# Transposes of two units share a pair of joined PSUM banks and one copy of 1024 columns

## The chip, the cores and the metric

The kernel runs on one core of a Trainium2 chip. A core has TensorE (PE in the profile; PEld is its weight load), VectorE (DVE), ScalarE (ACT), GpSimd (POOL) and SyncE (SP), which here only issues DMAs. Each engine runs its own list of instructions in order, and engines wait for one another by semaphores. The metric is the device time of one execution in microseconds (us); three runs of the kernel before gave 233.63, 234.40 and 234.79 us.

## The reference

Six residual layers on x, 16 batches x 32 tokens x 128 features: a local cross-attention, an RWKV-like recurrence, a small routed FFN, then the masked cross-attention in which the change lies, a linear attention with an FFN, and a mixture of 16 experts with a capacity. The masked cross-attention is, cut to its core:

```
qh, kh, vh = _split_heads(q @ Wq + bq), _split_heads(k @ Wk + bk), _split_heads(v @ Wv + bv)
scores = jnp.einsum('bhqd,bhkd->bhqk', qh, kh) * scale     # 16 batches, 16 heads, 32 queries, 512 keys
scores = scores + mask * NEG
weights = jax.nn.softmax(scores, axis=-1)
out = jnp.einsum('bhqk,bhkd->bhqd', weights, vh)
return out.transpose(0, 2, 1, 3).reshape(...) @ Wo + bo    # 128 features
```

## The kernel before, in words

**Units.** The cross-attention is cut into 64 units: 16 batches of 4 groups, each unit 4 heads x 32 queries (128 rows) by 512 keys. A unit goes through six steps:

- S, scores (L1406, PE): one matmul of 512 columns; a turn of the stream does the four units of a batch, into banks 0, 1, 2 and 5.
- least (L955, DVE): mask added, minimum taken, written to one of 8 tiles in SBUF.
- exponentials (L580, ACT): exp in place with its sum.
- T, turns (L1420, PE): four transposes of 128x128 into one PSUM bank, bank 3 for even units and bank 4 for odd ones.
- copies (L591 on ACT, L966 on DVE): the bank of 512 columns to one of 8 tiles `pt` in SBUF. Of every 8 units in turn, DVE copies those at 1, 4 and 7 and ACT the other five, so DVE copies 24 and ACT 40 in all.
- V, outputs (L1436, PE): 16 small matmuls for a batch, once its four units are copied.

The transposes of unit u wait for its exponential and for the copy of unit u-2, the last one that read the same bank. A copy waits for the transposes of its own unit, and for the batch whose V last read the `pt` tile. Before the cross-attention banks 3 and 4 serve the 32 projections of keys and values (L1235, L1239) in turn, and the first transposes wait until the last of these is copied.

**Order.** Every engine's list is woven from streams (Python generators): L the local attention, P the projections, a and b the two halves of the small layers, S, T and V as above (on DVE S is least, on ACT it is the exponentials, and T the copies on both), c and d the two halves of the later layers with the experts, G filler matmuls (L1650) that keep TensorE occupied near the end. `TURNS` is a table with one string for each engine: "T3" takes three turns of stream T. A turn of a stream that has ended does nothing. So the table decides what stands between two instructions of an engine, and nothing else does.

Of the kernel before, what the change touches and what calls it, by code (L numbers as in the profile page):

```python
# [6 lines left out]
F32 = mybir.dt.float32  # L7
# [4 lines left out]
P = 128  # L12
# [40 lines left out]
def columns(pack):  # L53

    at, out = 0, {}
    for name, n in pack:
# [10 lines left out]

TURNS = {
# [7 lines left out]
    "DVE": (  # L76
# [6 lines left out]
    "ACT": (  # L83
# [4 lines left out]
    "POOL": (  # L88
        "L2 a5 b a3 b a4 b10 c3 d c L a d c a c d2 L c d b d c b2 d b L a2 c L d2 ")}

# [26 lines left out]
def program(nc, x_d, early_d, next_d, late_d, ctx_d, ctok_d, mask_d, w1_d, w2_d, moeb_d, out_d):  # L117
    with ExitStack() as stack:
# [5 lines left out]
        def sig(name):  # L124
            if name not in sems:
                sems[name] = stack.enter_context(nc.semaphore(name))
            return sems[name]


        bank = [stack.enter_context(nc.psum_tensor(f"bank{i}", [P, 512], F32)) for i in range(8)]  # L130


        early, following, late = sb("early", width(EARLY)), sb("following", width(NEXT)), sb("late", width(LATE))
# [154 lines left out]

        def copied(j):

            part, n = j % 8, j // 8
            mine = part in BY_DVE
            before = sum(1 for k in range(part + 1) if (k in BY_DVE) == mine)
            return ("pT_dve", len(BY_DVE) * n + before) if mine else ("pT_act", (8 - len(BY_DVE)) * n + before)

        BY_DVE = (1, 4, 7)

        def taker(i):

# [172 lines left out]
        def _(act):  # L472
# [110 lines left out]

            def copies():

                for j in range(2 * UNITS):
                    if copied(j)[0] == "pT_act":
                        act.wait_ge(sig("pT_ps"), j + 1)
                        if j >= NPT:
                            act.wait_ge(sig("o1_ready"), (j - NPT) // GROUPS + 1)  # L590
                        s.copy(pt[j % NPT], bank[TB[j % 2]][:, :]).then_inc(sig("pT_act"), 1)  # L591
                        yield

            def linear_stages(h):
# [52 lines left out]
        def _(dve):  # L647
# [310 lines left out]

            def copies():

                for j in range(2 * UNITS):
                    if copied(j)[0] == "pT_dve":
                        dve.wait_ge(sig("pT_ps"), j + 1)
                        if j >= NPT:
                            dve.wait_ge(sig("o1_ready"), (j - NPT) // GROUPS + 1)
                        v.tensor_copy(pt[j % NPT], bank[TB[j % 2]][:, :]).then_inc(sig("pT_dve"), 1)  # L966
                        yield

            def take_heads():
# [226 lines left out]
        def _(pe):  # L1196
# [213 lines left out]
            def turns():  # L1410

                for u in range(2 * UNITS):
                    pe.wait_ge(sig("p1_ready"), u + 1)
                    if u < 2:
                        name, n = taker(len(PROJ) - 2 + u)
                    else:
                        name, n = copied(u - 2)
                    pe.wait_ge(sig(name), n)
                    for k in range(KT):
                        last = nc.tensor.transpose(bank[TB[u % 2]][:, P * k:P * (k + 1)], sc[u % NSC][:, P * k:P * (k + 1)], wt("ident"))  # L1420
                    last.then_inc(sig("pT_ps"), 1)
                    yield

            def outputs():

                for b in range(BATCH):
                    for j in range(GROUPS * b, GROUPS * (b + 1)):
                        name, n = copied(j)
                        pe.wait_ge(sig(name), n)
                    if b % 4 == 0 and b >= 4:  # L1430
# [323 lines left out]
```

## Time and profile before

| | us |
|---|---|
| median of three runs | 234.40 (233.63 to 234.79) |
| profiled execution | 233.0 |
| its span, first to last instruction | 231.2 |
| PE busy, share of the span | 217.0, 94% |
| DVE busy | 176.3, 76% |
| ACT busy | 131.7, 57% |
| granted TensorE clock, mean | 1.000 |

The span is 1.8 us shorter than the time of the same execution. The units of the cross-attention run from 89.2 us (the first S) to 181.4 us (the end of the last V), 92 of the 231 us; around and between them stand streams a and b up to about 133 us and stream c from about 136 us on. After them comes stream d, 50 us of small dependent steps.

### The profile page before, as it was taken

Reading aid. Unit: us, or ns where it says so; the run is one execution under the profiler, and the core shown is the slowest. Engines: PE = TensorE matmul, PEld = TensorE weight load, DVE = VectorE, ACT = ScalarE, POOL = GpSimd, SP = SyncE. Lnnn points to the kernel's source line nnn. Section 1 sums busy time; section 2 is a strip of 40 time slices with the busy share of each in tenths; the row PEclk is TensorE's granted clock in tenths of the full one; section 3 lists DMA queues with packets and bytes.
Section 4 is the critical chain, followed back from the end, with each engine's and each line's share of the span. In section 5 each row is a group of like instructions: output and inputs, shape, how many; then the busy total and the mean of one; then the engine's idle time right before and its main releaser. Section 6 shows DMA issues by size and latency. Waiting matters only on the chain.

```text
span 231.2 us, 5285 instructions
## 1 busy us (share of the span) xinstructions
PE 217.0 (94%) x1996; PEld 155.2 (67%) x1996; DVE 176.3 (76%) x507; ACT 131.7 (57%) x292; POOL 34.7 (15%) x55
## 2 busy tenths in 40 slices
PE   7999999999999998689899999999999989799995
PEld 6432785666876887355477766767677778688495
DVE  2476825999865799998798889999989777825672
ACT  2303452354488164889999979879969720123030
POOL 2020001050205137202050230020001031210000
DMA  6999979400000000007000520000009999200001
GB/s 217 396 420 463 403 292 230 89 3 0 4 0 0 3 0 1 0 3 181 3 0 4 135 52 0 3 3 1 3 3 346 404 428 412 96 0 0 3 3 45
DMA packets 2905, 26.88 MB, mean 116 GB/s; under 512 B 448, under 2 KB 704, under 8 KB 1344
## 3 DMA queue, kind: packets, MB, share of 16 engines
q1 hardware_dynamic: 2880, 26.54, 31.6%
q8 instruction: 16, 0.26, 0.5%
q14 instruction: 9, 0.07, 0.1%
HBM read 26.28 MB, written 0.26 MB: 115 GB/s over the span
## 4 chain that ended last, share of the span: by engine, by line
PE 74%; DVE 13%; issue 6%; ACT 3%; POOL 1%; POOLq 0%; DVEq 0%
PE bank L1420 11%; PE bank L1296 6%; PE bank L1274 6%; PE bank L1406 6%; PE bank L1436 5%; PE bank L1235 5%; PE bank L1239 3%; DVE ctx_sb L955 3%; PE bank L1246 2%; PE bank L1219 2%; PE bank L1650 2%; PE bank L1362 2%; PE bank L1379 2%; PE bank L1641 2%; PE bank L1263 2%
## 5 line engine op out<-in xcount | busy, mean ns | idle before, releaser
L580 ACT ACTIVATE ctx_sb<-ctx_sb,small_sb 128x512 f32<-128x512 f32 x64 | 45.9, 721 | 2.9 <-DVE small_sb L955 2.7
L955 DVE CUSTOM_DVE_ANT_0 ctx_sb<-bank,mask_sb 128x512 f32<-128x512 f32 x64 | 41.8, 682 | 2.6 <-PE bank L1406 1.4
L1420 PE MATMUL bank<-early_sb,ctx_sb 128*128 128x128 f32 x256 | 36.6, 278 | 2.8 <-DVE work_sb L966 1.8
L1420 PEld LDWEIGHTS bank<-early_sb,ctx_sb 128*128 128x128 f32 x256 | 28.0, 141 | 16.5 <-ACT ctx_sb L580 8.0
L382 POOL TENSOR_TENSOR rstd_sb<-veps_sb,minus_half_sb 128x2 f32<-128x2 f32 (+1 forms) x15 | 11.0, 734 | 125.7 <-DVE veps_sb L675 125.7
L591 ACT COPY work_sb<-bank 128x512 f32<-128x512 f32 x40 | 23.0, 580 | 8.1 <-PE bank L1420 8.0
L1406 PE MATMUL bank<-k_sb,work_sb 32*128 32x512 f32 x128 | 18.2, 638 | 2.3 <-DVE small_sb L955 1.8
L723 DVE SCALAR_TENSOR_TENSOR work_sb<-bank,early_sb,work_sb 128x512 f32<-128x512 f32 x16 | 11.8, 747 | 8.5 <-PE bank L1274 8.0
L1239 PEld LDWEIGHTS bank<-late_sb,ctx_sb 128*128 128x128 f32 x128 | 15.5, 191 | 3.4 <-issue 3.3
L1436 PE MATMUL bank<-work_sb,v_sb 128*32 128x128 f32 x512 | 17.1, 275 | 0.1
L1235 PE MATMUL bank<-ctx_sb,early_sb 128*128 128x512 f32 x32 | 16.3, 607 | 0.0
L966 DVE COPY work_sb<-bank 128x512 f32<-128x512 f32 x24 | 16.3, 681 | 0.1
L1239 PE MATMUL bank<-late_sb,ctx_sb 128*128 128x128 f32 x128 | 16.3, 278 | 0.0
L1274 PE MATMUL bank<-ctx_sb,early_sb 128*128 128x512 f32 x32 | 16.0, 605 | 0.3 <-DVE work_sb L723 0.2
L495 ACT ACTIVATE k_sb<-bank,early_sb 128x512 f32<-128x512 f32 x12 | 8.0, 685 | 14.1 <-PE bank L1235 14.1
L1436 PEld LDWEIGHTS bank<-work_sb,v_sb 128*32 128x32 f32 x512 | 13.2, 109 | 3.4 <-issue 1.7
L514 ACT COPY work_sb<-bank 128x512 f32<-128x512 f32 x16 | 9.3, 585 | 7.9 <-PE bank L1296 7.9
L580 ACT ACTIVATION_READ_ACCUMULATOR ctx_sb<-ctx_sb,small_sb 128x1 f32 x64 | 12.4, 193 | 0.0
L484 ACT ACTIVATE lnT_sb<-bank 128x256 f32<-128x256 f32 (+1 forms) x7 | 2.9, 413 | 14.4 <-PE bank L1205 14.3
L322 DVE TENSOR_TENSOR work_sb<-bank,early_sb 128x512 f32<-128x512 f32 x16 | 10.3, 678 | 0.8 <-PE bank L1283 0.7
L1650 PE MATMUL bank<-early_sb 128*128 128x128 f32 x64 | 10.0, 284 | 0.0
L1274 PEld LDWEIGHTS bank<-ctx_sb,early_sb 128*128 128x128 f32 x32 | 5.2, 189 | 6.5 <-issue 6.3
(264 smaller groups left out, 396.7 us busy)
## 6 DMA issues: line engine op xcount, KB each, us to landing
k_sb<-moe_w SPq DMA_DIRECT2D x1, 4096.0 KB, 13.5
ctx_sb<-moe_w SPq DMA_DIRECT2D x1, 4096.0 KB, 16.9
ctx_sb<-ctx SPq DMA_DIRECT2D x3, 1024.0 KB, 14.5
late_sb<-late SPq DMA_DIRECT2D x1, 2966.5 KB, 20.8
mask_sb<-ctx_tok SPq DMA_DIRECT2D x1, 2048.0 KB, 12.9
v_sb<-ctx_tok SPq DMA_DIRECT2D x1, 2048.0 KB, 28.2
mask_sb<-mask SPq DMA_DIRECT2D x4, 512.0 KB, 7.9
mask_sb<-mask SPq DMA_DIRECT2D x8, 256.0 KB, 4.5
```

The costliest lines, as they stand in the source:

```text
L580: s.activation(sc[u % NSC], sc[u % NSC], ACT.Exp, bias=smin[:, u:u + 1], scale=-1.0, accum_out=rsum[:, u:u + 1]).then_inc(sig("p1_ready"), 1)
L591: s.copy(pt[j % NPT], bank[TB[j % 2]][:, :]).then_inc(sig("pT_act"), 1)
L955: v.tensor_tensor_reduce(sc[u % NSC], bank[SB[u % GROUPS]][:, :], mask[:, KEYS * b:KEYS * (b + 1)], MASK_BIG, 3e38, ALU.add, ALU.min, smin ...
L966: v.tensor_copy(pt[j % NPT], bank[TB[j % 2]][:, :]).then_inc(sig("pT_dve"), 1)
L1235: last = mm(dst[:, :], wt("wk1"), ctx[:, KEYS * b:KEYS * (b + 1)], start=True, stop=True)
L1239: last = mm(dst[:, P * k:P * (k + 1)], ctx[:, at:at + P], wt("wv1"), start=True, stop=True)
L1274: mm(bank[c % 2][:, :], wt("wk0"), ctx[:, KEYS * c:KEYS * (c + 1)], start=True, stop=True).then_inc(sig("k0_ps"), 1)
L1296: last = mm(bank[c % 2][:, P * k:P * (k + 1)], ctok[h][:, at:at + P], mix[c % NE][:, P * k:P * (k + 1)], start=True, stop=True)
L1406: mm(bank[SB[g]][:, :], qc[b][r, :], k1[r, KEYS * b:KEYS * (b + 1)], start=True, stop=True)\
L1420: last = nc.tensor.transpose(bank[TB[u % 2]][:, P * k:P * (k + 1)], sc[u % NSC][:, P * k:P * (k + 1)], wt("ident"))
L1436: last = mm((bank[OB2][r, 0:P] if b == BATCH - 1 else bank[OB1][r, at:at + P]), vkey[:, b, k, r], pt[(GROUPS * b + g) % NPT][:, P * k:P * ...
L1650: mm(bank[2][:, 0:P], wt("ident"), early[:, 0:P], start=True, stop=True)
```

## The change

Banks 3 and 4 are allocated as one tensor `bank34` of 1024 columns, with the old names as its two halves. Two units (an even one and the next) form a pair. The transposes of the pair fill both halves; one operation of 1024 columns copies both to two neighbouring `pt` tiles. The choice of the copying engine goes by pairs: of 8 pairs in turn DVE takes those at 1, 4 and 6, so DVE has 12 copies and ACT 20. The first transposes of a pair wait for the copy of the pair before it; a copy waits for the transposes of both units. All four strings of `TURNS` are new.

```diff
 TURNS = {
     "PE": (
-        "P a2 b a3 b P2 b P b a P a P2 S L P2 S T5 S T V T b T S T3 V b T b S L T2 b S T b T V2 b T b S b T2 "
+        "b P a3 b P2 b P b a P a P2 S P2 S a T2 a T2 S T P T V T b T S T2 V T2 P b S b T2 V S T2 b2 V T b T b "
...
-        bank = [stack.enter_context(nc.psum_tensor(f"bank{i}", [P, 512], F32)) for i in range(8)]
+        bank = [stack.enter_context(nc.psum_tensor(f"bank{i}", [P, 512], F32)) for i in range(3)]
+        twin = stack.enter_context(nc.psum_tensor("bank34", [P, 1024], F32))
+        bank += [twin[:, 0:512], twin[:, 512:1024]]
+        bank += [stack.enter_context(nc.psum_tensor(f"bank{i}", [P, 512], F32)) for i in range(5, 8)]
...
         def copied(j):
-            part, n = j % 8, j // 8
+            part, n = j // 2 % 8, j // 16
...
-        BY_DVE = (1, 4, 7)
+        BY_DVE = (1, 4, 6)
...
             def copies():                                       # on ACT; on DVE likewise
-                for j in range(2 * UNITS):
+                for j in range(0, 2 * UNITS, 2):
                     if copied(j)[0] == "pT_act":
-                        act.wait_ge(sig("pT_ps"), j + 1)
+                        act.wait_ge(sig("pT_ps"), j + 2)
                         if j >= NPT:
-                            act.wait_ge(sig("o1_ready"), (j - NPT) // GROUPS + 1)
-                        s.copy(pt[j % NPT], bank[TB[j % 2]][:, :]).then_inc(sig("pT_act"), 1)
+                            act.wait_ge(sig("o1_ready"), (j + 1 - NPT) // GROUPS + 1)
+                        s.copy(tile(7 + j % NPT, 2), twin[:, :]).then_inc(sig("pT_act"), 1)
...
             def turns():
                 for u in range(2 * UNITS):
                     pe.wait_ge(sig("p1_ready"), u + 1)
-                    if u < 2:
-                        name, n = taker(len(PROJ) - 2 + u)
-                    else:
-                        name, n = copied(u - 2)
-                    pe.wait_ge(sig(name), n)
+                    if u % 2 == 0:
+                        for name, n in (copied(u - 2),) if u else (taker(len(PROJ) - 2), taker(len(PROJ) - 1)):
+                            pe.wait_ge(sig(name), n)
...
             def outputs():
                 for b in range(BATCH):
-                    for j in range(GROUPS * b, GROUPS * (b + 1)):
+                    for j in range(GROUPS * b, GROUPS * (b + 1), 2):
                         name, n = copied(j)
                         pe.wait_ge(sig(name), n)
```

What the new table puts on TensorE, first in the dense middle of the cross-attention, from the transposes of the 13th pair on. L1420 is a transpose (L1421 after), L1406 a score matmul (L1409), L1436 a V matmul (L1437), L1388 one matmul of stream b (L1391). Before:

```order
L1388 MATMUL bank7<-lnT_sb,late_sb 128x256
L1420 MATMUL bank4<-early_sb,ctx_sb 128x128 x4
L1420 MATMUL bank3<-early_sb,ctx_sb 128x128 x4
L1436 MATMUL bank6<-work_sb,v1_sb 32x128 x16
L1406 MATMUL bank0<-k1_sb,work_sb 128x512
L1406 MATMUL bank1<-k1_sb,work_sb 128x512
L1406 MATMUL bank2<-k1_sb,work_sb 128x512
L1406 MATMUL bank5<-k1_sb,work_sb 128x512
L1420 MATMUL bank4<-early_sb,ctx_sb 128x128 x4
L1420 MATMUL bank3<-early_sb,ctx_sb 128x128 x4
L1420 MATMUL bank4<-early_sb,ctx_sb 128x128 x4
L1436 MATMUL bank6<-work_sb,v1_sb 32x128 x16
```

and after:

```order
L1391 MATMUL bank7<-lnT_sb,late_sb 128x256
L1421 MATMUL bank34<-early_sb,ctx_sb 128x128 x8
L1409 MATMUL bank0<-k1_sb,work_sb 128x512
L1409 MATMUL bank1<-k1_sb,work_sb 128x512
L1409 MATMUL bank2<-k1_sb,work_sb 128x512
L1409 MATMUL bank5<-k1_sb,work_sb 128x512
L1421 MATMUL bank34<-early_sb,ctx_sb 128x128 x8
L1437 MATMUL bank6<-work_sb,v1_sb 32x128 x16
L1421 MATMUL bank34<-early_sb,ctx_sb 128x128 x8
```

Before, up to three units are transposed in a row, with the banks in turn; after, pairs of units alternate with one S or one V.

The second place is the end of the cross-attention on TensorE, behind the last S: L1525/L1526, L1219/L1222, L1205/L1208 and L1538/L1539 are steps of stream c. Before:

```order
L1406 MATMUL bank5<-k1_sb,work_sb 128x512
L1420 MATMUL bank3<-early_sb,ctx_sb 128x128 x4
L1219 MATMUL bank7<-late_sb,mask_sb 128x128 x2
L1420 MATMUL bank4<-early_sb,ctx_sb 128x128 x4
L1436 MATMUL bank6<-work_sb,v1_sb 32x128 x32
L1420 MATMUL bank3<-early_sb,ctx_sb 128x128 x4
L1420 MATMUL bank4<-early_sb,ctx_sb 128x128 x4
L1205 MATMUL bank7<-early_sb,xn_tok_sb 128x128 x2
L1420 MATMUL bank3<-early_sb,ctx_sb 128x128 x4
L1420 MATMUL bank4<-early_sb,ctx_sb 128x128 x4
L1538 MATMUL bank7<-lnT_sb,late_sb 128x256 x2
```

and after:

```order
L1437 MATMUL bank6<-work_sb,v1_sb 32x128 x16
L1421 MATMUL bank34<-early_sb,ctx_sb 128x128 x4
L1526 MATMUL bank7<-early_sb,mask_sb 128x128 x2
L1421 MATMUL bank34<-early_sb,ctx_sb 128x128 x4
L1222 MATMUL bank7<-late_sb,mask_sb 128x128 x2
L1421 MATMUL bank34<-early_sb,ctx_sb 128x128 x8
L1437 MATMUL bank6<-work_sb,v1_sb 32x128 x16
L1421 MATMUL bank34<-early_sb,ctx_sb 128x128 x4
L1208 MATMUL bank7<-early_sb,xn_tok_sb 128x128 x2
L1421 MATMUL bank34<-early_sb,ctx_sb 128x128 x4
L1539 MATMUL bank7<-lnT_sb,late_sb 128x256 x2
L1421 MATMUL bank34<-early_sb,ctx_sb 128x128 x8
```

The last S now stands earlier, with ten units still to transpose behind it instead of six, and between the last pairs stand L1222, one V and L1539.

## Rows read from the trace of the kernel before

**Rows 1.** The page: busy time of each engine, and the chain that ended last.
```profile
PE 217.0 (94%) x1996; PEld 155.2 (67%) x1996; DVE 176.3 (76%) x507; ACT 131.7 (57%) x292; POOL 34.7 (15%) x55
...
PE 74%; DVE 13%; issue 6%; ACT 3%; POOL 1%; POOLq 0%; DVEq 0%
```

**Rows 2.** Busy us (xinstructions) by stretch: PE, PEld, DVE, ACT, POOL, then clock.
```profile
90.00:100.00 10.00, 7.52 (x56) 4.58 (x52) 10.00 (x25) 7.15 (x18) 4.05 (x5) 1.00 0.01 2
100.00:110.00 10.00, 8.83 (x116) 6.29 (x112) 9.21 (x29) 8.76 (x24) 1.32 (x2) 1.00 0.43 105
110.00:120.00 10.00, 9.01 (x111) 5.95 (x111) 8.83 (x33) 9.90 (x20) 2.91 (x1) 1.00 0.01 2
120.00:130.00 10.00, 9.93 (x73) 7.38 (x72) 8.30 (x27) 9.58 (x23) 0.07 (x1) 1.00 0.05 11
130.00:140.00 10.00, 9.63 (x147) 7.12 (x144) 8.96 (x25) 8.72 (x22) 3.41 (x4) 1.00 0.42 100
140.00:150.00 10.00, 10.00 (x135) 7.04 (x137) 9.82 (x31) 9.15 (x26) 0.00 (x0) 1.00 0.01 2
150.00:160.00 10.00, 10.00 (x128) 7.29 (x132) 9.45 (x30) 8.54 (x23) 1.38 (x2) 1.00 0.01 2
160.00:170.00 10.00, 10.00 (x108) 6.57 (x108) 9.24 (x25) 9.23 (x25) 0.00 (x0) 1.00 0.01 2
170.00:180.00 10.00, 9.61 (x156) 7.63 (x148) 9.29 (x30) 7.65 (x19) 0.70 (x1) 1.00 0.55 211
```

**Rows 3.** The chain that ended last, in order: start us, us, what.
```profile
139.28 1.02 PE bank L1420 x8
140.30 1.07 PE bank L1406 x8
141.37 0.59 PE bank L1420 x4
141.96 1.01 PE bank L1436 x32
142.97 0.43 PE bank L1449 x8
...
146.97 0.45 PE bank L1462 x4
```

**Rows 4.** Groups by line: xcount | busy us, mean ns | idle before.
```profile
L591 ACT COPY work_sb<-bank 128x512 f32<-128x512 f32 x40 | 23.0, 580 | 8.1 <-PE bank L1420 8.0
L966 DVE COPY work_sb<-bank 128x512 f32<-128x512 f32 x24 | 16.3, 681 | 0.1
```

**Rows 5.** One line each: min/median/max ns of the nearest other widths.
```profile
L600 ACT COPY mask_sb<-bank x1: 372/372/372, 189.8 to 189.8; 128x256 f32<-128x256 f32 x1
L620 ACT ACTIVATE mask_sb<-mask_sb x1: 1057/1057/1057, 184.3 to 184.3; 128x1024 f32<-128x1024 f32 x1
L1065 DVE COPY mask_sb<-bank x2: 415/420/424, 172.8 to 194.8; 128x256 f32<-128x256 f32 x2
```

**Rows 6.** Timeline: start us, us, engine, line, what, [idle before <-releaser].
```profile
101.64 0.68 DVE L966 COPY work_sb<-bank 128x512 f32<-128x512 f32 x1
...
102.47 0.63 PE L1420 MATMUL bank<-early_sb,ctx_sb 128*128 128x128 f32 x4 [0.80 <-DVE work_sb L966]
...
136.91 0.59 ACT L591 COPY work_sb<-bank 128x512 f32<-128x512 f32 x1 [0.40 <-PE bank L1420]
...
137.64 0.63 PE L1420 MATMUL bank<-early_sb,ctx_sb 128*128 128x128 f32 x4 [0.33 <-ACT work_sb L591]
...
138.30 0.59 ACT L591 COPY work_sb<-bank 128x512 f32<-128x512 f32 x1 [0.81 <-PE bank L1420]
138.78 0.73 ACT L580 ACTIVATE ctx_sb<-ctx_sb,small_sb 128x512 f32<-128x512 f32 x1
...
140.36 0.68 DVE L966 COPY work_sb<-bank 128x512 f32<-128x512 f32 x1
...
140.96 0.41 DVE L998 TENSOR_TENSOR mask_sb<-late_sb,small_sb 128x256 f32<-128x256 f32 x1
...
148.80 1.09 PE L1420 MATMUL bank<-early_sb,ctx_sb 128*128 128x128 f32 x8
...
150.18 0.66 DVE L966 COPY work_sb<-bank 128x512 f32<-128x512 f32 x1
```

**Rows 7.** Timeline: the short steps of stream c, and the last V.
```profile
155.79 0.65 PE L1470 MATMUL bank<-lnT_sb,late_sb 128*128 128x256 f32 x2
...
156.27 0.61 PE L1219 MATMUL bank<-late_sb,lnT_sb 128*128 128x128 f32 x4
...
182.25 1.10 PE L1538 MATMUL bank<-lnT_sb,late_sb 128*128 128x256 f32 x4 [0.17 <-ACT mask_sb L615]
...
183.18 0.61 PE L1457 MATMUL bank<-late_sb 128*128 128x128 f32 x4
```

**Rows 8.** What PE waited for, 120 to 181 us: us, times, longest.
```profile
PE bank L1420 <- DVE work_sb L966: 0.3, 1, 0.3
PE bank L1420 <- ACT work_sb L591: 0.3, 1, 0.3
```

More of the change, by code:

```diff
@@ L69 @@
     "PE": (
[6 rows of a table removed]
-    "DVE": (
[6 rows of a table removed]
[6 rows of a table added]
+    "DVE": (
[6 rows of a table added]
     "ACT": (
[4 rows of a table removed]
[4 rows of a table added]
     "POOL": (
-        "L2 a5 b a3 b a4 b10 c3 d c L a d c a c d2 L c d b d c b2 d b L a2 c L d2 ")}
+        "L a L a5 b a2 b a3 b a b L b5 L b3 c2 b L c d a L c d c d c d a b d a c2 d c L b c a b d b d3 a ")}
 class Shifted:
@@ L959, in copies @@
             def copies():
-                for j in range(2 * UNITS):
+                for j in range(0, 2 * UNITS, 2):
                     if copied(j)[0] == "pT_dve":
-                        dve.wait_ge(sig("pT_ps"), j + 1)
+                        dve.wait_ge(sig("pT_ps"), j + 2)
                         if j >= NPT:
-                            dve.wait_ge(sig("o1_ready"), (j - NPT) // GROUPS + 1)
-                        v.tensor_copy(pt[j % NPT], bank[TB[j % 2]][:, :]).then_inc(sig("pT_dve"), 1)
+                            dve.wait_ge(sig("o1_ready"), (j + 1 - NPT) // GROUPS + 1)
+                        v.tensor_copy(tile(7 + j % NPT, 2), twin[:, :]).then_inc(sig("pT_dve"), 1)
                         yield
```

30 rows, old and new, of the table TURNS are left out of this document.

## The prediction, made before the changed kernel ran

> **What bounds the kernel now.** I read the page first. PE is busy for 94% of the span and holds 74% of the chain that ended last [rows 1]. Such an average hides that stages differ, so next come the stretches of 10 us in the 92 us of cross-attention [rows 2]. From 90 to 120 us PE is idle for 2.48 + 1.17 + 0.99 = 4.6 us, while DVE is full in the first of the three: this part hangs on stream b's recurrence. From 120 to 180 us PE is idle for 0.07 + 0.37 + 0.39 = 0.8 us in all. DVE (8.3 to 9.8 of 10) and ACT (7.7 to 9.6) are close behind, but the chain shows which ends last: PE follows PE with no wait between [rows 3]. So from 120 us on TensorE is the bound, and time in which it stands before a transpose is lost. Whatever delays the last V delays stream d, whose first steps take its result. The granted clock is 1.00 in every stretch [rows 2], TensorE's upper level of 2.4 GHz, and the change takes no filler away.
>
> **The change, part by part.**
>
> *Copies.* The trace has no copy of 1024 columns, so I bound it. On ACT 256 columns take 0.372 us and 512 take 0.580, 0.21 for 256 more, so 1024 should take 0.58 + 0.42 = 1.00; the one ACT operation of 1024 columns took 1.06 [rows 4, 5]. On DVE 0.420 and 0.681 give 0.681 + 0.52 = 1.20. Between that and two copies lie 1.00 to 1.16 for ACT and 1.20 to 1.36 for DVE; below these an operation would have to run faster per column than any row of its engine. I take 1.01 and 1.21, near the slopes. By durations that saves ACT 20 x (1.16 - 1.01) = 3.0 us and DVE 12 x (1.36 - 1.21) = 1.8 us. The engines gain less: the next exponential starts 0.48 us after a copy of 0.59 starts, the next DVE operation 0.60 after a copy of 0.68 [rows 6], so the last 0.1 us lies beside the next operation anyway. In engine time a pair saves 2 x 0.48 - (1.01 - 0.11) = 0.06 on ACT and 2 x 0.60 - (1.21 - 0.08) = 0.07 on DVE, 1.2 and 0.8 us in all. About four DVE copies lie where DVE bounds: -0.3 us. The rest goes to engines that don't end last.
>
> The Trainium skill (Perfetto Trace Analysis, Optimizing Scalar/DVE Operations) advises larger operations where the engine is saturated, with a busy overhead on PSUM of some 125 ns for DVE and 51 ns for ScalarE. By it, as an estimate, DVE would gain 12 x 0.125 = 1.5 us and ACT 20 x 0.051 = 1.0 us; the trace agrees on ACT and shows about half of it on DVE.
>
> *The banks.* This is the costly part. Before, unit u waits for the copy of u-2, so a copy lies beside the transposes of the unit between. After, both banks are held until one long copy is done, and only S, V and the small streams can fill the gap. Eight transposes take PE 1.02 us up to the next step [rows 3]; the last one ends 1.09 us after the first starts (the eight at 148.80) and a free copier starts 0.03 us behind that (137.64 + 0.63 to 138.30) [rows 6]. PE resumes 0.14 us behind an ACT copy (137.50 to 137.64) and 0.15 behind one of DVE (102.32 to 102.47) [rows 6]. From the first transpose of a pair to the first of the next it takes at least 1.09 + 0.03 + 1.01 + 0.14 = 2.27 us by ACT, 1.09 + 0.03 + 1.21 + 0.15 = 2.48 by DVE. So the gap between two pairs must hold 2.27 - 1.02 = 1.25 us of other PE work with ACT and 1.46 with DVE. S gives 1.07 and V 1.01 [rows 3]: S alone is short by 0.18 with ACT and 0.39 with DVE, V alone by 0.24 and 0.45.
>
> The new PE order has 31 such gaps. Fourteen hold enough (S and V together, or one with work of b or c). The first five are empty, S, V, S, V with copiers ACT, DVE, ACT, ACT, DVE: 1.25 + 0.39 + 0.24 + 0.18 + 0.45 = 2.5 us short. They lie at about 95 to 110 us, where PE idles 4.6 us for stream b; I count them as hidden, and as +2.5 if that cover is gone. The other twelve lie behind 125 us:
> - S alone, twice with ACT and three times with DVE: 0.36 + 1.17;
> - V alone, four times with ACT: 0.96;
> - L1391 alone, with ACT; its cover is 0.48 us as of L1470's row [rows 7]: 0.77;
> - L1222 alone, with DVE; 0.45 us as of L1219, here 156.27 to 156.72: 1.01;
> - L1539 alone, with DVE; 0.93 us as of L1538, 182.25 to 183.18 [rows 7]: 0.53.
>
> The sum is 4.8 us, of which the 0.8 us that PE was idle there before may take its part: +4.0. A step of PE that stands alone costs a bit more than in a row: a lone unit takes 0.59 us, two together 1.02 [rows 3], 0.07 less for each. By the two orders nine lone units behind 125 us become four: -0.3 us.
>
> *End of the cross-attention.* The last V needs the last pair's copy, and behind the last S there are now ten units instead of six. PE's total work is the same, so I cost this at nothing beyond the gaps above, which include the last two. Streams L, P, a, the first S and all of d have the same work in almost the same order; I take 0, and +-1 us for an order made anew.
>
> Sum: -0.3 + 4.0 - 0.3 = +3.4; on the profiled execution's own 233.0 that is 236.4 us. The median of the runs is 1.4 above that execution, so I forecast 234.4 + 3.4 = 237.8.
>
> The skill's same page (Matmuls) says that independent groups should rotate through PSUM banks so that the evacuation of one lies beside the next group's matmuls. The trace agrees in its copies that lie beside transposes. By this rule a pair without rotation loses its whole copy, minus what else PE has to do, which is the sum above.
>
> **Rivals.**
>
> *Faster: the copies were the bound.* From 140 to 170 us DVE is 92 to 98% busy and ACT 85 to 92% [rows 2], and PE's place in the chain may hang on how they keep up. If what ends last is DVE's queue and the new order puts enough S and V into the gaps, the whole 1.8 us of durations come off: 234.4 - 1.8 = 232.6, at most 3.0 by ACT's share, 231.4. It decides if PE stands before transposes no longer than before. For it: the balance of the three engines, and 4.6 us of PE idle that another order could use. Against it: PE has no wait in the chain from 139 to 147 us [rows 3], and engine time gains less than durations.
>
> *Much slower: the copier is not free.* Copies stand in order behind exponentials of 0.72 us or a DVE operation. Before, the DVE copy behind the eight transposes at 148.80 started at 150.18, 0.29 us after their end at 149.89 [rows 6]. With two banks this cost nothing; now each of the twelve gaps pays it: 12 x 0.3 = 3.6 more, 241.3.
>
> *No change: the gaps are covered.* If PE's idle 0.8 us, the first third's 4.6 and the relief of DVE and ACT take up the gaps, it stays at 234.4. That also holds if the loop of transposes and copies is seldom the last wait, because the exponential of the pair comes later than the copy of the one before.
>
> **How the numbers follow.** Forecast, +1.2 to +5: 0.42. Copier not free: 0.20. No change: 0.13. Faster: 0.25. About 0.5% (1.2 us) is what a measurement can tell from no change. So faster 0.25, same 0.13, slower 0.62. The likeliest case alone has 235.6 to 239.5. The range reaches into both others: down to 231.8, which takes in most of the faster case, and up to 242.0, past 241.3.
>
> **What would show it.** Right: PE idle time before the transposes, released by the copies, grows from 0.3 + 0.3 us behind 120 us [rows 8] to 4 or more, the largest before lone L1391, L1222 and L1539; copies of 1.01 and 1.21 us; the last V ends 3 us later, and stream d takes 50 us as before. Wrong: PE idles no more than before in that stretch; or copies start late, and the gaps are 0.3 us longer each; or the first five gaps come on top of stream b's idle time; or the last V comes on time and the end moves by stream d.

## The result, and the profile after

The changed kernel takes 240.84 us (median of four runs, 239.24 to 242.41), the kernel before beside it 234.59 (four runs, 233.63 to 239.77). The ratio is 1.028, 95% interval 1.019 to 1.037. The forecast was 237.8 us, range 231.8 to 242.0: the sign and the range were right, the size was 3 us too small (2.2 us at equal clock, below).

One thing must be known to read the sizes. Executions of either kernel differ in TensorE's mean granted clock, and the time goes with it (1.00 stands for 0.999 and more, 0.993 for 0.992 and 0.993): over the runs beside the experiments the kernel before has a median of 234.1 us at 1.00 (23 runs, 232.8 to 234.9), 235.9 at 0.993 (20 runs) and 237.9 at 0.978 (13 runs). At 1.00 the changed kernel has 239.7 (five runs, 239.2 to 240.3), which is 5.6 us over before; at 0.993 it has 241.5 (three runs, 241.4 to 242.4), again 5.6 over, where the forecast had 3.4. Single runs at one clock spread by 1 to 2 us, so differences of such medians are good to about 1 us, not to tenths. Below, "at 1.00" means such runs alone. The profiled execution of after has 0.993, that of before 1.00.

The page of the changed kernel, the lines of [rows 1] and [rows 4] (columns as there):

```profile
PE 222.8 (93%) x2008; PEld 158.4 (66%) x2008; DVE 177.0 (74%) x495; ACT 131.1 (54%) x272; POOL 34.5 (14%) x55
...
PE 57%; DVE 21%; issue 12%; ACT 4%; DMA 3%; POOL 2%; SPq 0%; DVEq 0%; POOLq 0%
...
L1421 PE MATMUL bank<-early_sb,ctx_sb 128*128 128x128 f32 x256 | 35.0, 277 | 5.0 <-ACT work_sb L594 2.7
...
L594 ACT COPY work_sb<-bank 128x1024 f32<-128x1024 f32 x20 | 20.1, 1006 | 10.6 <-PE bank L1421 10.4
...
L969 DVE COPY work_sb<-bank 128x1024 f32<-128x1024 f32 x12 | 14.7, 1222 | 1.2 <-PE bank L1421 1.1
```

The copies are cheaper in busy time, 20.1 us on ACT instead of 23.0 and 14.7 on DVE instead of 16.3. But the chain is no longer three quarters PE: DVE's share of it went from 13 to 21%, and the issue share from 6 to 12%. The copiers wait longer for PE before their copies, ACT 10.4 us instead of 8.0 [rows 4] for half as many copies, DVE 1.1 instead of next to nothing: they are not late themselves.

What PE waited for, 120 to 190 us (us, times, longest), beside [rows 8]:

```profile
PE bank L1421 <- ACT work_sb L594: 1.2, 5, 0.5
...
PE bank L1421 <- DVE work_sb L969: 1.1, 3, 0.6
```

Before it was 0.3 + 0.3 us; now it is 2.3. (This is less than what the gaps cost, as shown below the experiments.) The next view is the timeline of after where three pairs follow each other with one S or V between:

```profile
140.89 1.06 PE L1421 MATMUL bank<-early_sb,ctx_sb 128*128 128x128 f32 x8
...
141.89 1.08 PE L1437 MATMUL bank<-work_sb,v_sb 128*32 128x128 f32 x32
142.00 1.01 ACT L594 COPY work_sb<-bank 128x1024 f32<-128x1024 f32 x1 [0.18 <-PE bank L1421]
...
143.15 1.06 PE L1421 MATMUL bank<-early_sb,ctx_sb 128*128 128x128 f32 x8 [0.18 <-ACT work_sb L594]
...
144.26 1.22 DVE L969 COPY work_sb<-bank 128x1024 f32<-128x1024 f32 x1 [0.88 <-PE bank L1421]
...
145.40 0.34 DVE L994 RECIPROCAL small_sb<-small_sb 128x32 f32<-128x32 f32 x1
...
145.63 1.06 PE L1421 MATMUL bank<-early_sb,ctx_sb 128*128 128x128 f32 x8 [0.34 <-DVE work_sb L969]
```

From transposes to transposes it is 143.15 - 140.89 = 2.26 us where ACT copies and 145.63 - 143.15 = 2.48 where DVE does; the forecast had 2.27 and 2.48. DVE even stood idle 0.88 us for the transposes, and stream c's reciprocal (L994, L991 before) was queued behind that copy.

Where the 9.4 us between the two profiled spans went is best read from stretches cut at the same events in each: first projection, first S, L1388 of stream b's last part (L1391 after), last S, last V, end. Each row has the stretch, its length, then busy us (xinstructions) of PE, PEld, DVE, ACT, POOL, the granted clock, and the DMA share with GB/s. Before:

```profile
6.42:89.16 82.74, 81.96 (x497) 53.77 (x497) 59.87 (x141) 38.30 (x73) 13.30 (x26) 1.00 0.44 158
89.16:132.60 43.44, 38.72 (x396) 26.40 (x396) 39.42 (x121) 38.36 (x88) 10.54 (x10) 1.00 0.17 42
132.60:172.30 39.70, 39.34 (x508) 28.07 (x508) 37.21 (x109) 33.66 (x87) 3.45 (x4) 1.00 0.05 11
172.30:180.55 8.25, 7.85 (x108) 5.87 (x108) 7.86 (x26) 7.62 (x19) 0.70 (x1) 1.00 0.82 320
180.55:231.20 50.65, 44.11 (x480) 37.19 (x480) 30.28 (x105) 12.23 (x26) 4.85 (x7) 1.00 0.35 147
```

and after:

```profile
8.64:92.64 84.00, 82.83 (x496) 53.35 (x497) 59.93 (x137) 38.35 (x73) 13.00 (x20) 1.00 0.41 149
92.64:137.30 44.66, 39.65 (x393) 27.61 (x393) 38.20 (x115) 36.95 (x79) 10.42 (x10) 0.96 0.17 41
137.30:175.60 38.30, 35.49 (x436) 24.65 (x436) 34.30 (x97) 31.55 (x73) 3.45 (x4) 1.00 0.05 11
175.60:190.59 14.99, 13.63 (x179) 10.03 (x180) 11.75 (x32) 11.99 (x25) 0.70 (x1) 1.00 0.75 296
190.59:240.60 50.01, 45.40 (x492) 38.42 (x492) 30.29 (x105) 10.78 (x22) 4.84 (x7) 1.00 0.27 112
```

- 2.2 us lie ahead of the first projection, which waits for the first context DMA: 8.64 against 6.42. In the other profiled executions it starts at 6.8 to 8.4 us, with old and new tables, so at least part of this is this execution's own.
- 1.26 us lie between first projection and first S, before any transpose of the cross-attention.
- 6.56 us lie between first S and last V (97.95 against 91.39). PE's idle time in it, length less busy, rises from 4.72 + 0.36 + 0.40 = 5.48 to 5.01 + 2.81 + 1.36 = 9.18 us, by 3.7.
- The tail is 0.64 us shorter.

The busy time of the same stretch rises by 2.9 us with 1,008 records against 1,012. About 1 us of this is the clock. Sixteen matmuls of stream b (L1382) took the time below in a stretch at 0.87, where the same step (L1379) had 2.2 us in the execution before. But the run rotate below, with the same table and records and a clock of 1.00, has 38.56 + 35.30 + 13.89 = 87.75 us of busy time against 85.91 before: 1.8 us come with the new order, in which TensorE's steps lie less tightly behind each other. After also has 12 more matmul records than before, all of them filler (L1650), in the last 50 us.

```profile
129.47 3.56 PE L1382 MATMUL bank<-late_sb,mask_sb 128*128 128x128 f32 x16
```

### The profile page after: what moved, and what is told of

It reads as the page before. It is cut to its first block, busy times and chain, and to the rows that moved or that the text cites. A ratio compares the mean times of both kernels' runs of the same rounds, so it can differ in the third digit from the quotient of the medians.

```text
span 240.6 us, 5201 instructions
## 1 busy us (share of the span) xinstructions
PE 222.8 (93%) x2008; PEld 158.4 (66%) x2008; DVE 177.0 (74%) x495; ACT 131.1 (54%) x272; POOL 34.5 (14%) x55
## 4 chain that ended last, share of the span: by engine, by line
PE 57%; DVE 21%; issue 12%; ACT 4%; DMA 3%; POOL 2%; SPq 0%; DVEq 0%; POOLq 0%
PE bank L1421 7%; PE bank L1299 6%; DVE ctx_sb L958 6%; PE bank L1409 5%; PE bank L1277 5%; PE bank L1238 4%; PE bank L1651 3%; DMA ctx_sb<-ctx 3%; ACT work_sb L594 2%; DVE work_sb L969 2%; PE bank L1539 2%; PE bank L1437 2%; PE bank L1552 2%; PE bank L1642 2%; PE bank L1308 2%
## 5 line engine op out<-in xcount | busy, mean ns | idle before, releaser
L1421 PEld LDWEIGHTS bank<-early_sb,ctx_sb 128*128 128x128 f32 x256 | 27.9, 141 | 18.9 <-issue 9.7
L1421 PE MATMUL bank<-early_sb,ctx_sb 128*128 128x128 f32 x256 | 35.0, 277 | 5.0 <-ACT work_sb L594 2.7
L594 ACT COPY work_sb<-bank 128x1024 f32<-128x1024 f32 x20 | 20.1, 1006 | 10.6 <-PE bank L1421 10.4
L1409 PE MATMUL bank<-k_sb,work_sb 32*128 32x512 f32 x128 | 18.5, 638 | 2.4 <-DVE small_sb L958 1.4
L1437 PE MATMUL bank<-work_sb,v_sb 128*32 128x128 f32 x512 | 17.3, 275 | 0.2 <-ACT work_sb L594 0.2
L969 DVE COPY work_sb<-bank 128x1024 f32<-128x1024 f32 x12 | 14.7, 1222 | 1.2 <-PE bank L1421 1.1
L1437 PEld LDWEIGHTS bank<-work_sb,v_sb 128*32 128x32 f32 x512 | 13.1, 109 | 2.8 <-issue 2.6
L517 ACT COPY work_sb<-bank 128x512 f32<-128x512 f32 x16 | 9.1, 585 | 7.8 <-PE bank L1299 7.8
L1651 PE MATMUL bank<-early_sb 128*128 128x128 f32 x76 | 10.8, 280 | 0.0
L1651 PEld LDWEIGHTS bank<-early_sb 128*128 128x128 f32 x76 | 9.7, 192 | 0.2
## 6 DMA issues: line engine op xcount, KB each, us to landing
mask_sb<-ctx_tok SPq DMA_DIRECT2D x1, 2048.0 KB, 14.7
```

Of the source, the lines that this page charges most:

```text
L594: s.copy(tile(7 + j % NPT, 2), twin[:, :]).then_inc(sig("pT_act"), 1)
L969: v.tensor_copy(tile(7 + j % NPT, 2), twin[:, :]).then_inc(sig("pT_dve"), 1)
L1409: mm(bank[SB[g]][:, :], qc[b][r, :], k1[r, KEYS * b:KEYS * (b + 1)], start=True, stop=True)\
L1437: last = mm((bank[OB2][r, 0:P] if b == BATCH - 1 else bank[OB1][r, at:at + P]), vkey[:, b, k, r], pt[(GROUPS * b + g) % NPT][:, P * k:P * ...
L1651: mm(bank[2][:, 0:P], wt("ident"), early[:, 0:P], start=True, stop=True)
```

## The experiments

Theory A: the loop through the held banks is the cost (the forecast's sum). Rival B: the new order costs, whatever the banks do. Rival C: an engine, DVE above all, is the bound. Intervals are of the ratio to before.

**after_again.** The changed kernel once more, beside the next three.

> The changed kernel once more, for the spread of its own runs and for the granted clock. In its first profile the first context slice landed about 2.2 us later than before, and the clock fell to 0.96 and 0.87 in two stretches around 120 to 140 us. If both are chance of that execution, this profile starts its projections at about 7.5 us as before, keeps clock 1.00 and ends near 237 us of span (time 239); if the late start belongs to the kernel, it shows again, with 240 us or more. In either case the cross-attention, first S to last V, takes 95 to 98 us instead of 91.4.

Measured: 239.89 us, ratio 1.021 (1.014 to 1.027). Its stretches repeat to 0.02 us (84.00, 44.64, 38.30, 14.99, 50.01), the clock's dip included. So the loss is steady; only the start of the first projection (7.76) moved. The dip came again, the late start only in part.

**rotate.** After's table and order; each pair is copied by two operations of 512 on one engine, and each bank is free after its own.

```diff
-                        s.copy(tile(7 + j % NPT, 2), twin[:, :]).then_inc(sig("pT_act"), 1)
+                        for i in (j, j + 1):
+                            act.wait_ge(sig("pT_ps"), i + 1)
+                            s.copy(pt[i % NPT], bank[TB[i % 2]][:, :]).then_inc(sig("pT_act"), 1)
...
-                    if u % 2 == 0:
...
+                    name, n = copied(u - 2) if u > 1 else taker(len(PROJ) - 2 + u)
+                    pe.wait_ge(sig(name), n)
```

> The new table of turns is kept word for word; each pair's copy of 1024 columns is made as two of 512 by the same engine, and the transposes of unit u wait for the copy of u-2 only, so the two banks rotate again. Theory (banks held through one long copy bound the pairs' loop): PE's waits before transposes released by copies fall from 4.7 us to under 1.5, the cross-attention shrinks by 3 to 5 us, and the time comes to 235 to 237. Rival (the new order itself is worse, the banks don't matter): 239 to 241, with the same length of cross-attention as the changed kernel.

**split_only.** The same two copies, but the banks stay a pair: no transpose before both copies are done.

```diff
-                        for name, n in (copied(u - 2),) if u else (taker(len(PROJ) - 2), taker(len(PROJ) - 1)):
+                        for name, n in (copied(u - 1),) if u else (taker(len(PROJ) - 2), taker(len(PROJ) - 1)):
```

> The new table is kept; each pair's copy is made as two operations of 512 columns, both after the transposes of both units, and PE waits for both as in the changed kernel: no rotation. It prices the single operation alone. By the rows before, ACT holds the pair 0.48 + 0.59 = 1.07 us instead of 1.01 and DVE 0.60 + 0.68 = 1.28 instead of 1.22: theory, 0.06 us more in each of some 17 short gaps, +1 us against the changed kernel, 240 to 242. A rival by which the wide operation is what helps (the durations of 3.0 and 1.8 us): +2 to +4 us.

Measured: rotate 238.74 us, ratio 1.013 (1.006 to 1.021), at 1.00 238.1 us (three runs, 238.0 to 239.4); split_only 244.33, ratio 1.027 (1.018 to 1.036), at 1.00 241.7 (two runs). Rotate lies between theory (235 to 237) and rival (239 to 241). So the joined copy over held banks costs 239.7 - 238.1 = 1.6 us, and with the copy cut in two and the banks still held it is 3.6: the one wide operation is worth 2.0 us as long as the banks are held. Split_only's timeline accounts for these 2.0, which the expectation put at 1. From transposes to transposes it is 2.38 us by ACT (141.35 to 143.73) and 2.60 by DVE (143.73 to 146.33), 0.12 more than in after: 0.06 for the longer copying, as expected, and 0.06 because the copy starts that much later. Over the 17 short gaps this is 2.0. But 4.0 of the 5.6 us stay when the banks rotate. Rotate's groups and stretches:

```profile
L1423 PE MATMUL bank<-early_sb,ctx_sb 128*128 128x128 f32 x256 | 35.9, 278 | 0.7 <-ACT work_sb L596 0.6
...
L1412 PE MATMUL bank<-k_sb,work_sb 32*128 32x512 f32 x128 | 18.6, 638 | 4.1 <-DVE small_sb L960 2.8 <-POOL work_sb L412 1.1
```

```profile
8.28:92.28 84.00, 82.83 (x497) 53.38 (x497) 59.92 (x137) 38.35 (x73) 13.00 (x20) 1.00 0.41 149
92.28:135.50 43.22, 38.56 (x393) 26.04 (x393) 38.43 (x119) 37.31 (x86) 10.42 (x10) 1.00 0.18 42
135.50:172.95 37.45, 35.30 (x437) 24.71 (x437) 34.45 (x103) 32.23 (x83) 3.45 (x4) 1.00 0.05 12
172.95:187.60 14.65, 13.89 (x178) 10.09 (x179) 11.84 (x34) 11.75 (x28) 0.70 (x1) 1.00 0.80 312
187.60:237.60 50.00, 45.37 (x492) 38.42 (x492) 30.25 (x105) 10.78 (x22) 4.85 (x7) 1.00 0.26 110
```

The transposes (L1423) hardly wait, 0.7 us against 2.8 before and 5.0 after. Yet PE's idle time from first S to last V is 4.66 + 2.15 + 0.76 = 7.57, still 2.1 over before: it stands before S instead (4.1 us, before 2.3), for the minimum of the batch before (L960) and for POOL. With the 1.8 us of busy time this makes the 3.9 us by which this stretch is longer than before. The front keeps its 84.00.

**old_order_pairs.** Before's table with joined banks and joined copies: a pair's copy stands in the turn in which before copied the pair's later unit on that engine, and DVE takes pairs 0, 3 and 6 of eight to fit that table. The main lines:

```diff
-        bank = [stack.enter_context(nc.psum_tensor(f"bank{i}", [P, 512], F32)) for i in range(8)]
+        twin = stack.enter_context(nc.psum_tensor("bank34", [P, 1024], F32))
...
-        BY_DVE = (1, 4, 7)
+        BY_DVE = (0, 3, 6)
```

> The table of the kernel before, with joined banks and one copy of 1024 columns for a pair; ACT and DVE take a pair's copy where they took the copy of its last unit of theirs, DVE the pairs 0, 3 and 6 of 8 (a third of its places needed a new owner). Theory: an order made for rotating banks has gaps emptier still, with pairs back to back, so it is slower than the changed kernel, 242 to 248. Rival (the banks cost nothing and the order made anew costs): 234 to 237.

Measured: 264.17 us, ratio 1.124 (1.116 to 1.132), at mean clocks of 0.961 to 0.974. The direction is theory's, the size is not: 16 us above its range of 242 to 248. Some of it is the clock, which no run of this kernel had at 1.00. PE's waits over the whole run, then its timeline in the middle:

```profile
PE bank L1421 <- ACT work_sb L594: 11.9, 12, 1.2
PE bank L1421 <- DVE work_sb L969: 9.8, 11, 1.7
```

```profile
137.85 1.06 PE L1421 MATMUL bank<-early_sb,ctx_sb 128*128 128x128 f32 x4
140.11 1.09 PE L1421 MATMUL bank<-early_sb,ctx_sb 128*128 128x128 f32 x4 [1.19 <-ACT work_sb L594]
```

An order made for rotating banks puts the next transposes right behind a pair; every such gap is empty and costs a whole copy, here 1.19 us. So the joined copy needs another order, and the new one brings its 21.7 us of bank waits down to 4.7. What this order costs by itself is the next question.

**old_front and new_front.** Old_front is after with before's table up to the first S on PE, DVE and ACT (POOL's string stays); new_front is before with after's front, likewise. Such a line of PE's table, in new_front:

```diff
-        "L P L P L11 P4 L P L8 P L2 a L P L2 a P L a2 L a L P L P L2 P6 a L P2 L P L2 a L a2 L P L P L2 a L a "
+        "L P L P L11 P4 L P L8 P L2 a L P L2 a P L a3 L2 P L2 P L P5 a P L P L3 a P L a L2 P a L2 a P2 a L a2 "
```

> The changed kernel, but on each engine the table up to its first turn of S is that of the kernel before; behind it stand the new table's turns that are not yet taken. In four profiles of kernels with the new front the first scores start 84.00 us after the first projection, in the kernel before 82.74. Theory (the new front alone costs 1.3 us): 82.7 again, and 1.3 us less than the changed kernel, 238.5. Rival (joined banks 3 and 4 slow the projections, or it is chance): 84.0 and 239.9.

> The kernel before, but on each engine the table up to its first turn of S is the new one. Mirror of the run before it: by the theory 84.0 us from the first projection to the first scores and 235.8 us of time against 234.5 to 235.5, ratio 1.005; by the rival 82.7 and no change.

Measured: old_front 239.23 us, ratio 1.019 (1.011 to 1.027), at 1.00 238.3 (three runs, 237.9 to 238.7); new_front 235.76, ratio 1.003 (0.998 to 1.008), at 1.00 235.1 (seven runs, 234.4 to 236.0). Taking the new front out of after gives back 1.4 us, putting it into before costs 1.0 (1.2 at 0.993, four runs). The interval of new_front's ratio holds 1, so alone it wouldn't prove the step; the two together do. The stretch from first projection to first S agrees: 84.00 with the new front in after, after_again and rotate, 83.94 in new_front, 82.74 in before. Old_front's own stretch can't be used, as its profiled execution had a clock dip there.

**rotate_old_front.** Rotate with before's front: new order of the rest alone.

> The kernel with rotating banks and the new table, with the old table's front. If the three parts simply add (front 1.3, rotation 1.2 to 2, the rest of the new order 2 to 4), this is 237.4 us, still slower than before by 0.8 to 1.5%, and what is left is the order of the cross-attention's second half. A rival by which the front and the rotation are all: 235, same as before.

Measured: 240.55 us, ratio 1.016 (1.005 to 1.028); five of its six runs had a clock of 0.993 or lower, three of them 0.979. The one at 1.00 took 236.4, 2.4 over before; the one at 0.993 is 3.4 over before's 235.9, and the three at 0.979 are 3.3 over its 237.9. The sum 5.6 - 1.2 - 1.6 = 2.8 lies between. So the rest of the new order costs 2.4 to 3.4 us.

**narrow_copy and narrow_copy_before.** Only the middle 256 of 1024 columns of a pair are copied (of 512, the middle 128 before); all instructions and waits stay.

```diff
-                        s.copy(tile(7 + j % NPT, 2), twin[:, :]).then_inc(sig("pT_act"), 1)
+                        s.copy(tile(7 + j % NPT, 2)[:, 384:640], twin[:, 384:640]).then_inc(sig("pT_act"), 1)
```

> The changed kernel with each pair's copy cut to the middle 256 of its 1024 columns (three quarters of the transposed weights are not copied); order and waits unchanged. The hold of the banks falls by about 0.6 us on ACT and 0.8 on DVE, and the copies' engine time by 12 and 9 us. Theory by which long copies on both banks are the larger part: -4 to -6 us, PE's idle time before transposes nearly gone, and the cross-attention shorter than with narrow copies in the kernel before. Rival (the new order ties TensorE to the minimum operation on DVE and to stream c): -2 to -3 us, with PE still waiting for the minimum before scores.

> The kernel before with each copy cut to the middle 128 of 512 columns, the same three quarters left out. TensorE has no wait in its chain from 120 to 172 us, so by the prediction's reading hardly anything is gained behind 120 us and at most 1 to 2 us in the first third: 233 to 234.5. If the copies' engine time bounded (the rival of the prediction), -5 us or more.

Measured: narrow_copy 236.42 us, ratio 1.006 (1.002 to 1.010), at 1.00 236.3 (seven runs, 234.8 to 236.6), 3.3 below after. Narrow_copy_before 233.80, ratio 0.996 (0.992 to 1.001), at 1.00 232.8 (three runs), 1.3 below before. ACT's copy of 256 columns has a mean of 0.369 us (x20), 0.64 less than the wide one; so the length of a copy is worth 2.0 us more in after than in before. The transposes' wait falls to 0.6 us, while S still waits for the minimum, as the rival had it. This agrees with rotate: what depends on how long the banks are held is some 2 us, and over 2 us are left even with short copies, of which the front is about half.

**narrow_least and narrow_least_before.** DVE's minimum over 256 of 512 columns, in after and in before.

```diff
-                    v.tensor_tensor_reduce(sc[u % NSC], bank[SB[u % GROUPS]][:, :], mask[:, KEYS * b:KEYS * (b + 1)], MASK_BIG,
+                    v.tensor_tensor_reduce(sc[u % NSC][:, 0:256], bank[SB[u % GROUPS]][:, 0:256], mask[:, KEYS * b:KEYS * b + 256], MASK_BIG,
```

> The changed kernel with the mask-and-minimum operation on DVE cut to 256 of its 512 columns (half of each unit's scores are left out); the rest as it is. DVE is relieved by 64 x 0.27 = 17 us and the scores' banks come free 0.27 us earlier each. Theory (the new order hangs on DVE where TensorE waits for the minimum before each S): -4 to -6 us. Rival (the copies are what holds TensorE): -2 us or less.

> The same cut in the kernel before. There TensorE bounds from 120 us on, so only the first third, where DVE carries stream b's recurrence, can gain: -2 to -3 us, less than in the changed kernel. If both gain alike, the dependence on DVE is no part of the difference.

Measured: narrow_least 237.85 us, ratio 1.011 (1.004 to 1.018), at 1.00 237.8 (three runs, 236.0 to 237.9), 1.9 below after. Narrow_least_before 235.34, ratio 0.997 (0.992 to 1.002); none of its runs had a clock of 1.00. At 0.992 to 0.993 it has a median of 233.4 (four runs, 233.0 to 234.7), 2.5 below before's 235.9. Both kernels win about 2 us from a faster DVE, so both hang on DVE in places, and rival C explains none of the difference. In narrow_least S no longer waits for the minimum; 0.6 us of waiting for POOL is left.

**rotate_tail.** The last look at the order: in rotate's table the last V stands 3.3 us behind stream c's L1538 (1.05 before). Here the last pair's transposes go ahead of that matmul and its copies ahead of ACT's table load.

```diff
-        "T2 c V T2 V T2 c S c T2 S c T2 c V L T c T P S c T S T V T P c T c S T2 V2 d c b d2 c d2 G d2 c b G2 "
+        "T2 c V T2 V T2 c S c T2 S c T2 c V L T c T P S c T S T V T2 c T2 c P S V2 d c b d2 c d2 G d2 c b G2 "
...
-        "c S4 T c3 T L c b S L P S3 P T S4 a T S4 b S T S c3 T S c4 T d2 c d2 b2 d c S d7 T c d P S T d6 c2 a "
+        "c S4 T c3 T L c b S L P S3 P T S4 a T S4 b S T S c T c2 S c4 T d2 c d2 b2 d c S d7 T c d P S T d6 c2 "
```

> The kernel of run rotate (the changed kernel's table, each joined pair copied out by two operations of 512 columns of one engine, banks rotating) with the last part of the table changed: on TensorE the last pair's transposes stand ahead of stream c's first FFN matmul (L1541 in the numbers of before) and the pair before it stands ahead of L1211; on ScalarE the last pair's copies stand right behind c's L488, ahead of the activation table load and of L620. Theory A (part of what remains over before is the place of the last pair in the table, which puts the last V some 3.3 us behind stream c's L1538 where before it came 1.05 behind): the last V starts about 2 us earlier relative to L1538, the tail behind it stays at 50.0, and at granted clock 1.00 the time is 235.5 to 236.5 us, against 238.1 for rotate and 234.3 for before. Rival B (the end is set by stream c's own chain or by the loop over the transposes, not by this place): no change, 237.7 to 239 us. Rival C (the copies put ahead of the table load hold back stream c's own chain, and the tail grows by what is won): 237 to 238.5 with the last V earlier and the stretch behind it longer than 50.0.

Measured: 241.36 us, ratio 1.026 (1.020 to 1.032); the one run at 1.00 has 239.2, above rotate's 238.1. The timeline shows why:

```profile
184.35 0.76 DVE L1004 TENSOR_TENSOR mask_sb<-late_sb,small_sb 128x256 f32<-128x256 f32 x2
...
185.03 1.28 DVE L972 COPY work_sb<-bank 128x512 f32<-128x512 f32 x2
...
185.86 1.22 PE L1423 MATMUL bank<-early_sb,ctx_sb 128*128 128x128 f32 x8 [1.42 <-DVE work_sb L972]
...
186.92 1.03 PE L1541 MATMUL bank<-lnT_sb,late_sb 128*128 128x256 f32 x4
```

The transposes now stand ahead of L1541 on PE and wait 1.42 us for a DVE copy that is queued behind two steps of stream c; L1541, whose input was there, waits with them. The last V came no earlier (97.5 us behind the first S, rotate 95.3; some of it is a clock dip as in after). None of the three forecasts held. So moving the last pairs forward in PE's and ACT's lists, with DVE's left as it is, doesn't help. Whether all three moved together would was not tried.

## Why the forecast was right in sign and range, and short in size

*The copies*, 1.01 and 1.21 us: measured 1.006 and 1.222. Right; so was the reading that a pair saves next to nothing of engine time. The Trainium skill's rule on grouping (Perfetto Trace Analysis, Optimizing Scalar/DVE Operations) would have given a gain on saturated engines. By split_only against after the wide copy is worth 2.0 us here, and 17 gaps that are each 0.12 us shorter account for it: it comes through the bank loop, not through DVE's or ACT's load.

*The loop*, 2.27 and 2.48 us with one S or V short by 0.18 and more: right to 0.01 us.

*The twelve gaps behind 125 us*: their sum of 4.8 us was right, the step from it to the time was not. Start to start (a pair's first transpose to the next pair's, less 1.02 us for the eight transposes, or 0.59 for a last unit that stands alone, and less S's, V's or the small step's own time) they come to 4.65 us: 0.34 and 1.18 behind S with ACT and with DVE, 0.94 behind V, 0.73 behind L1391, 0.97 behind L1222 and 0.49 behind L1539. The 2.3 us of listed waits show only half of it: four gaps are not listed, and in the others the end of the matmul before counts as busy (V's row lasts 1.08 us, the step behind it can start after 1.01). Thus from L1222 to the transposes it is 1.33 us, of which the step covers 0.45, so 0.88 are lost; the row has 0.62:

```profile
182.05 0.71 PE L1222 MATMUL bank<-late_sb,mask_sb 128*128 128x128 f32 x4
...
183.38 1.06 PE L1421 MATMUL bank<-early_sb,ctx_sb 128*128 128x128 f32 x8 [0.62 <-DVE work_sb L969]
```

In rotate, where no bank is held, the same twelve gaps still come to 2.7 us, since PE waits there for something else:

```profile
137.93 1.14 PE L1412 MATMUL bank<-k_sb,work_sb 32*128 32x512 f32 x8 [0.76 <-POOL work_sb L412]
...
146.64 1.14 PE L1412 MATMUL bank<-k_sb,work_sb 32*128 32x512 f32 x8 [0.38 <-DVE small_sb L960]
...
151.59 1.14 PE L1412 MATMUL bank<-k_sb,work_sb 32*128 32x512 f32 x8 [0.31 <-DVE small_sb L960]
```

So holding the banks adds 1.9 us to them, near the 1.6 between the two kernels. The forecast charged all 4.8 us to the banks, less the 0.8 that PE was idle in the old order. The right thing to take off was what PE would wait in the new order, and that is the 2.7. The forecast named this case (its rival "no change", where the loop is seldom the last wait), but left it out of the sum.

*The first five gaps*, counted as hidden under stream b: PE waits 1.5 + 0.9 us for copies between 92 and 125, before 0.6 + 1.5. Right.

*The order made anew, put at 0, give or take 1 us*: this step failed. The front took 1.0 to 1.4 us, shown by old_front and new_front. The rest of the order took 2.4 to 3.4, shown by rotate_old_front at three clocks and by the difference. Together they are 4.0 us by rotate against before, 70% of the loss, where the forecast had nothing. The forecast read the order only for gaps between transposes, and took "the same work in almost the same order" for "the same time". The order of the stream steps counted more: in rotate PE idles 2.1 us more from first S to last V though its transposes hardly wait, most of it before S, for DVE's minimum and for POOL. Its busy time rises by 1.8 us there, where the forecast had 0.3 less for fewer lone units.

*The end*: "the last V ends 3 us later, stream d takes 50 us as before". Stream d did (50.01; 50.65 before). From first S, the last V came 6.6 us later in the profiled execution, 3.9 in rotate. In after the last S stands at 175.60 and fifteen microseconds of pairs and stream c follow it, where before it was eight. The chain of after there, in time (start us, us, what):

```profile
182.01 1.24 DVE work_sb L969
183.25 0.14 issue
183.38 1.08 PE bank L1421 x8
184.46 0.02 issue
184.48 1.02 ACT work_sb L594
185.50 0.14 issue
185.64 0.63 PE bank L1421 x4
```

Here copy and transposes alternate with nothing between that could cover the copy: the loop itself ends last, as the forecast had it.

*The rivals.* "Copier is not free": against it stands that ACT and DVE wait for PE before their copies (10.4 and 1.1 us), and the loop has its smallest length in the middle. "Faster" fell: DVE's load is nothing that this change relieves. The forecast's 237.8 was thus made of a term too large by 2.4 (4.0 where rotate has 1.6) and one missing of 4.0. The sign would have held by the banks alone; that the size came within 3 us is luck in part, as the two errors offset each other.

What stays open: which of the moved steps cost the 2.4 to 3.4 us. The traces show that stream c starts later (L991 3.5 us behind L1388 before, 8.1 behind L1391 in after, 7.5 in rotate), queued behind minima and a copy on DVE. In narrow_least, where the minima are half as wide, it is still 8.1 us behind, so their length is not what sets it. That this delay is the cause was not tested alone, and moving the one place that rotate_tail tried did not help.

No kernel here that does the whole work beats before. The best with after's idea is rotate at 238.1, which drops the joined copy.

## What to carry to other kernels

A wider copy out of PSUM over joined banks saves almost nothing of engine time, and takes from TensorE the bank in which it could go on: work out the loop (transposes, copy, hand-over both ways) against the work that stands between two pairs, and expect the sum of the shortfalls as an upper bound (4.65 us in the gaps here, 1.6 in the time), since in part of the gaps something else would be late as well. An order made for rotating banks can't be kept (+30 us here, some of it at a lower clock), and the order that replaces it has a price of its own, here larger than the banks' (4.0 against 1.6 us). So when a change brings a new order, run the new order without the change first, and cost the moved steps of every stream, not only of the one that the change is about.

## What the runs showed of the hardware

Without any change of the kernel, the mean granted clock differs from one execution to the next, and each step of the mean clock from 1.00 to 0.993 to 0.978 cost 1.8 and 2.0 us of 234. In the profiled executions a dip lies near 76 to 86 us or near 124 to 134 (old_order_pairs has others besides), and in it the clock is at its lower level of 1.2 GHz. The dip near 80 us came in five of the six profiled executions with the old front and in none of the eight with the new one; why is open. After, in stretches of 10 us (columns as in [rows 2]):

```profile
120.00:130.00 10.00, 9.34 (x80) 6.68 (x81) 8.07 (x24) 9.94 (x19) 2.05 (x1) 0.96 0.01 2
130.00:140.00 10.00, 9.27 (x88) 7.33 (x90) 6.85 (x23) 6.82 (x16) 2.45 (x4) 0.87 0.46 106
140.00:150.00 10.00, 9.18 (x120) 5.70 (x115) 8.64 (x23) 7.68 (x18) 1.02 (x1) 1.00 0.01 2
```

PE was busy 9.3 of 10 us in the dips and 9.2 in the stretch that followed at 1.00; rotate has 9.5 and 9.2 in the same two stretches and no dip. So the busy share of the stretch itself does not tell the two apart, and what sets it off in one execution and not in another stays open. Old_order_pairs, with the most idle time of PE, had it in all its runs (0.961 to 0.974). Medians of few runs with mixed clocks mislead by up to 2 us: narrow_least_before could only be judged at equal clock.
